# Transposing a row-scaled kernel matrix as two fp16 parts, with fewer warming products and one norm product

## The reference

```python
W = adj * adj
x = layernorm(x + einsum('bnf,nm->bmf', x, W) + bias)      # first layer; its result is called h below

z_l = h @ W_lang.T;  z_g = h @ W_grav.T;  v = h @ W_V.T     # second layer
zn  = z_l / max(norm(z_l), EPS)
A_l = max(zn @ zn.T, 0) * not_eye
A_g = exp(-d2(z_g) / (2 * sigma * sigma)) * not_eye         # d2: squared distances, at least 0
K   = w_l * row_stochastic(A_l * mask) + (1 - w_l) * row_stochastic(A_g * mask)
x   = layernorm(h + (K @ v) @ W_O.T)
```

## Time and profile before

| | |
|---|---|
| time, median of 3 runs | 602.76 us (602.34 to 603.36) |
| the profiled execution, its own time | 602.72 us |
| its span in the profile | 600.9 us |
| PE busy | 588.3 us (98%) |
| PEld busy | 314.3 us (52%) |
| DVE busy | 466.2 us (78%) |
| ACT busy | 275.8 us (46%) |
| POOL busy | 206.3 us (34%) |
| granted TensorE clock, mean of the span | 0.996 |
| first load of x_in, issued and landed | 3.84 us and 10.6 us after the start |

### The profile page before, as it was taken

One profiled execution on the slowest core, in us unless ns is written; L12 is line 12 of the kernel. 1 busy time (PEld: TensorE's weight loads), 2 busy tenths in 40 slices (PEclk: granted clock), 3 DMA queues, 4 the chain that ended last, 5 costly groups with the idle time before them and its releaser, 6 DMA issues.

```text
span 600.9 us, 14104 instructions
## 1 busy us (share of the span) xinstructions
PE 588.3 (98%) x5554; PEld 314.3 (52%) x5554; DVE 466.2 (78%) x964; ACT 275.8 (46%) x473; POOL 206.3 (34%) x200
## 2 busy tenths in 40 slices
PE   9999899999999999999999999999999999999993
PEld 6544555555464555546455555546455555546451
DVE  1756778787878878787887878787887878786775
ACT  2544434445435454444445454544545444533543
POOL 1221604334350624425260523525161533414011
PEclk9999999999999999999999999999999999999998
DMA  8660232324434342233434242233434230314103
GB/s 264 202 183 1 58 85 37 105 86 58 140 70 140 61 123 60 81 103 61 140 70 140 52 111 72 58 126 70 140 70 140 44 96 20 55 71 71 71 2 140
DMA packets 89401, 55.19 MB, mean 92 GB/s; under 512 B 70816, under 2 KB 70816, under 8 KB 89376
## 3 DMA queue, kind: packets, MB, share of 16 engines
q1 hardware_dynamic: 89376, 54.84, 33.3%
HBM read 21.27 MB, written 16.78 MB: 63 GB/s over the span
## 4 chain that ended last, share of the span: by engine, by line
PE 97%; DVE 1%; ACT 1%; issue 0%; POOLq 0%; POOL 0%; ACTq 0%
PE proj L406 35%; PE proj L424 28%; PE front L383 8%; PE ps_t L438 8%; PE ps_v L451 3%; PE ps_t L458 3%; PE ps_k L488 2%; PE front L488 2%; PE proj L572 2%; PE proj L604 2%; PE ps_v L469 2%; PE ps_t L572 1%; PE ps_k L367 1%; PE ps_t L604 1%; PE front L501 0%; DVE stats L937 0%
## 5 line engine op out<-in xcount | busy, mean ns | idle before, releaser
L630 ACT ACTIVATE p_hi<-proj 128x512 f16<-128x512 f32 x128 | 76.1, 595 | 120.1 <-PE proj L406 119.2
L1156 POOL TENSOR_TENSOR x_lo<-x_in,x_hi 128x512 fp32r<-128x512 f32 x60 | 78.6, 1322 | 97.9 <-ACT x_hi L620 97.9
L424 PE MATMUL proj<-m_hi,ht_hi 128*64 128x512 f16 x512 | 98.6, 382 | 0.0
L424 PE MATMUL proj<-m_lo,ht_hi 128*64 128x512 f16 x512 | 97.9, 379 | 0.0
L424 PE MATMUL proj<-m_hi,ht_lo 128*64 128x512 f16 x512 | 97.9, 379 | 0.0
L816 DVE TENSOR_TENSOR p_lo<-proj,p_hi 128x512 f16<-128x512 f32 x128 | 85.8, 680 | 13.5 <-ACT p_hi L630 13.4
L1150 POOL TENSOR_TENSOR ve<-mv,eps_ln 128x4 f32<-128x4 f32 x31 | 12.1, 391 | 166.8 <-DVE mv L789 164.5
L635 ACT ACTIVATE uv<-proj 128x512 f16<-128x512 f32 x64 | 38.1, 595 | 52.5 <-PE proj L424 52.1
L406 PE MATMUL proj<-ht_hi,l_lang_hi 128*128 128x512 f16 x160 | 61.1, 382 | 0.0
L406 PE MATMUL proj<-ht_hi,l_grav_hi 128*128 128x512 f16 x160 | 61.1, 382 | 0.0
L667 ACT ACTIVATE o<-o,nmr,rstd 128x512 f32<-128x512 f32 x60 | 47.0, 808 | 30.1 <-DVE nmr L897 29.7
(11 more groups left out here) (186 smaller groups left out, 1207.7 us busy)
## 6 DMA issues: line engine op xcount, KB each, us to landing
x_in<-in_x SPq DMA_DIRECT2D x16, 1024.0 KB, 6.7
out<-o SPq DMA_DIRECT2D x15, 1024.0 KB, 5.2
w_raw_lang<-in_L_gnn_W_lang SPq DMA_DIRECT2D x4, 256.0 KB, 3.5
o<-in_L_gnn_W_O SPq DMA_DIRECT2D x1, 1024.0 KB, 9.9
w_raw_grav<-in_L_gnn_W_grav SPq DMA_DIRECT2D x4, 256.0 KB, 9.9
uv<-in_L_gnn_W_V SPq DMA_DIRECT2D x1, 1024.0 KB, 12.0
ht_hi<-h_hi SPq DMA_TRANSPOSE x64, 2.5
ht_lo<-h_lo SPq DMA_TRANSPOSE x64, 2.5
```

The lines of the kernel that those rows point to most:

```text
L424: mm = pe.matmul(proj[j % 3][q * N:(q + 1) * N, :], a[g.parity][:, k, rows:rows + N], b[:, k, :], start=(n == 0), stop=(n == len(passes) - 1))
L630: act.activation(p_hi[:, j % 4, :, j // 4, :], by_batch(proj[j % 3]), ACT.Copy).then_inc(phi_ready, 1)
L1156: pool.tensor_tensor(x_lo[:, p, :], x_in[g.parity][:, p, :], x_hi[:, p, :], ALU.subtract).then_inc(xlo_ready, 1)
```

## The change

There are three edits. `WARM_START` goes from 10 to 5. The four accumulating norm products of M become one product with four columns, and DVE adds the four sums before it clamps. And in all groups but the last, `ks_sb` is split into fp16 parts, `ks_hi` on ACT (`ks_high`) and `ks_lo` on DVE (`rows_low`), and `kernel_t` transposes the two parts with fp16 products that accumulate; it waits for the low part. The last group, in `back`, keeps the fp32 products under the name `last_kernel_t`.

```diff
-WARM_START = 10
+WARM_START = 5
...
+        ks_hi = sb("ks_hi", [P, ROWS], F16)
+        ks_lo = sb("ks_lo", [P, ROWS], F16)
+        eye2_16 = sb("eye2_16", [P, N], F16)
...
-            def kernel_t(g):
+            def last_kernel_t(g):
 
                 pe.wait_ge(ks_ready, g.count(1, 1))
                 for b in (0, 2, 1, 3, 4, 6, 5, 7):
                     p, q = b // 4 * 2 + b % 2, b // 2 % 2
                     mm = pe.matmul(ps_v[q * N:(q + 1) * N, p * N:(p + 1) * N],
                                    ks_sb[:, b * N:(b + 1) * N], eye2[:, :], start=True, stop=True)
                 mm.then_inc(kt_done, 1)
 
+            def kernel_t(g):
+
+                pe.wait_ge(kslo_ready, g.count(1, 1))
+                for n, part in enumerate((ks_hi, ks_lo)):
+                    for b in (0, 2, 1, 3, 4, 6, 5, 7):
+                        p, q = b // 4 * 2 + b % 2, b // 2 % 2
+                        mm = pe.matmul(ps_v[q * N:(q + 1) * N, p * N:(p + 1) * N],
+                                       part[:, b * N:(b + 1) * N], eye2_16[:, :],
+                                       start=(n == 0 and b in (0, 2)), stop=(n == 1), skip_group_check=True)
+                mm.then_inc(kt_done, 1)
...
             def back(g):
-                kernel_t(g)
+                last_kernel_t(g)
...
                     pe.wait_ge(norm_copied, 1)
-                    for k in range(DC):
-                        mm = pe.matmul(ps_k[:, 2:3], ones[:, :], ssq[:, 2 + k:3 + k], start=(k == 0), stop=(k == DC - 1))
-                    mm.then_inc(norm_done, 1)
+                    pe.matmul(ps_k[:, 2:2 + DC], ones[:, :], ssq[:, 2:2 + DC], start=True, stop=True).then_inc(norm_done, 1)
...
+            def ks_high(g):
+                act.wait_ge(ks_ready, g.count(1, 1))
+                act.activation(ks_hi[:, :], ks_sb[:, :], ACT.Copy).then_inc(kshi_ready, 1)
...
                 p_high(g, 1, first)
+                if has_prev:
+                    ks_high(before)
                 p_high(g, 2, first)
...
+            def rows_low(g):
+                dve.wait_ge(kshi_ready, g.count(1, 1))
+                dve.tensor_tensor(ks_lo[:, :], ks_sb[:, :], ks_hi[:, :], ALU.subtract).then_inc(kslo_ready, 1)
...
             def m_scale():
                 dve.wait_ge(norm_done, 2)
-                dve.tensor_scalar(ssq_all[:, 2:3], ps_k[:, 2:3], TINY, None, ALU.max).then_inc(norm_copied, 1)
+                dve.reduce_sum(ssq_all[:, 2:3], ps_k[:, 2:2 + DC], X_AXIS).then_inc(norm_copied, 1)
+                dve.wait_ge(norm_copied, 2)
+                dve.tensor_scalar(ssq_all[:, 2:3], ssq_all[:, 2:3], TINY, None, ALU.max).then_inc(norm_copied, 1)
...
                 p_low(g, 1)
+                if has_prev:
+                    rows_low(before)
                 p_low(g, 2)
...
             dve.tensor_copy(eye_g[:, :], ident[:, N:P]).then_inc(dve_const, 1)
+            dve.tensor_copy(eye2_16[:, :], eye2[:, :])
...
                 if not has_prev:
-                    pool.wait_ge(norm_copied, 2)
+                    pool.wait_ge(norm_copied, 3)
```

More of the change, by code:

```diff
@@ L248, in resnorm_graph_kernel @@
         ks_ready = sem("ks_ready")
+        kshi_ready = sem("kshi_ready")
+        kslo_ready = sem("kslo_ready")
         kt_done = sem("kt_done")
```

## The result

| | before | after |
|---|---|---|
| time, median of 6 runs | 602.69 us (601.93 to 603.36) | 598.78 us (598.38 to 599.58) |
| the profiled execution, its own time | 602.72 us | 599.46 us |
| its span | 600.9 us | 597.6 us |

The ratio is 0.9938, with a 95% interval of 0.9925 to 0.9951: 3.9 us faster, where 4.3 were forecast (598.4).

What follows compares the result with a forecast made beforehand. The prediction took PE's instruction list to bound the kernel. Its terms, -3.6 (steady iterations), +0.9 (last iteration), -0.7 (norm) and -0.9 (start), sum to -4.3 against 602.72 us: 598.4 us, range 597.2 to 602.6.

Steps and rivals of the forecast that it cites:

- PE's list bounds the kernel: Whole kernel: the chain is 97% PE, so a us taken out of PE's list is a us of the time.
- The 16 fp16 products take half: `kernel_t`: half of 0.52 us, 0.26 us saved for each group, -3.6 us over 14 steady iterations.
- the first rival: `kernel_t`: the pace of the pairs stays, the steady gain goes, 602.3 us; chance 0.18.
- The two new steps hide in the steady iterations: `ks_high` on ACT and `rows_low` on DVE end before PE reaches `kernel_t`: margin 0.18 us, wait 0.
- The last iteration loses 0.9: Last iteration's `kernel_t`: PE waits 1.2 us for the low part, less 0.26 saved, +0.9 us.
- The norm gives 0.7: Norm of M, ahead of `project(0)`: 6 of 8 PE instructions go, -0.7 us.
- The warming products give 0.9: Start: PE begins W_lang's first block earlier, the level rising at the same moment, about 5.4 us: -0.9 us.
- the fourth rival: Start: the level rises later, +0.5 us for the start, all else as forecast, 599.8 us; chance 0.14.
- The sum: All terms against the profiled execution's 602.72 us: -4.3 us, so 598.4 us.

Runs made afterwards that it cites:

- late_low: The changed kernel with `rows_low` behind `p_low(2)` in DVE's list rather than ahead of it: 611.79 us, ratio 1.0157 to before.
- last_fp32_warm_6: The changed kernel with the last iteration's transposition in fp32 again and six warming products rather than five: 598.58 us, ratio 0.9925 to before.
- warm_only: The kernel before with `WARM_START` 5 rather than 10 and nothing else: 602.20 us, ratio 0.9990 to before.
- undo_warm: The changed kernel with `WARM_START` back at 10: 599.99 us, ratio 0.9958 to before.
- changed_again: The changed kernel itself, unaltered, run again on another chip: 599.01 us, ratio 0.9943 to before.
- fp32_unpaired: The kernel before with the blocks of its fp32 `kernel_t` in the order (0, 1, 4, 5, 2, 3, 6, 7): 608.03 us in a single execution.

## Why the prediction was right, point by point

- **PE's list bounds the kernel**: right. Every us of the result can be read as a us of that list: fewer transposition steps, fewer norm steps, an earlier start, one wait.
- **The 16 fp16 products take half**: right, and the first rival is out. They take 0.25 us against some 0.47. The term was mis-sized a little: -3.15 us and not -3.6. I put 0.10 of the 0.62 us down to the gap behind the products, and halved 0.52. The eight pairs of before are 8 x 0.058 = 0.47, and the gap behind fp32 products is about 0.15; the eight pairs of fp16 are 8 x 0.032 = 0.25, and some 0.12 is left of the gap. The weight load's row, 110 ns against 137, and 110 to 113 in the changed kernel, was the right one to go by. Whether the load or the product set the pace of 0.058 in fp32 is argued from the earlier trace rows, and no run separates the two. The Trainium skill's rule in "TensorE: Matmul & The Clock Gate", "LDWEIGHTS (loading the stationary operand)", gives 53 ns for these loads. Here a pair of loads and products passes every 0.032 us, so for 64 fp16 columns the measurement decides against it. The Trainium skill's floor of some 25 ns between starts ("TensorE: Matmul & The Clock Gate", under "Wait — 56ns, not 53.3ns?") doesn't hold across two halves either: 16 products start within 0.25 us.
- **The two new steps hide in the steady iterations**: right. The room forecast was 0.18 us, and 0.2 is there; `late_low` shows that this wait is the one that decides, and that it was thin.
- **The last iteration loses 0.9**: right, 0.97, and `last_fp32` gives it back.
- **The norm gives 0.7**: right, 0.66. DVE's second small instruction cost nothing that shows: ACT's `p_high(0)` now follows on M's split without idle time, and the first `gram`'s wait of 1.5 us is the same.
- **The warming products give 0.9**: right on average, not in a single execution. I assumed that the level rises at 5.4 us in both kernels. By the spacing of the products it rose at 5.6, 6.4, 6.9, 7.1 and 7.3 us in the five profiles with ten warming products (mean 6.7), and at 5.8 to 7.3 in the seven with five (mean 6.6). So 5.4 was not the moment, but the two kernels do share one on average, and that is all that the term needs: W_lang's first block starts 1.9 us earlier (3.57 and 5.48), so 1.9 us more of it run at half speed ahead of the rise, and that is half of 1.9 us of its work, 0.95, wherever the rise is. The 7.0 against 6.4 us that the expectation of `last_fp32_warm_6` starts from come from the lengths of the first block, which with five products hold the first load's delay and the last product's tail as well. By the spacing there was no later rise to explain. The first layer of group 0 starts at 15.12 on average in the former (14.62 to 15.42), at 14.15 in the latter (13.66 to 14.57): 0.97 us. The profile of before happened to be the earliest of its kind, which is why the two profiles differ by 0.43 only: between these two the fourth rival, a later rise, came near (599.46 us, where it had 599.8). That the averages agree so well with so few profiles, each spread over 0.8 to 0.9 us, is in part luck. In the times, `warm_only` gives 0.4, `undo_warm` against the changed kernel 1.0 to 1.2 (on other chips).
- **The sum**: -3.15 + 0.97 - 0.66 - 0.97 = -3.8, measured -3.9, and -3.4 with `changed_again` on another chip (medians). The forecast of -4.3 was high by the transposition's half us.

What stays open: the executions of one kernel spread over 0.7 to 1.7 us. Between the two profiled ones of the changed kernel the start is all that differs (583.4 us from the first layer to the end in both), but it isn't shown that it explains the whole spread. The profile of before has the earliest rise of its kind, and yet that execution took 602.72 where the fastest took 601.88. By the start alone that would need a rise 1.7 us earlier, at 3.9 us (an estimate, twice the 0.84 us), and no profile shows one before 5.6. Why the moment varies is open too.

A version better than both kernels comes out of it: `last_fp32`, the change with the last iteration's transposition left in fp32, at 598.40 and 598.15 us (0.9930 and 0.9921 of before). That it is better than the changed kernel rests on the marks (0.96 us), not on the medians.

## What to carry to other kernels

A step inserted into a full pipeline costs what its consumer waits, not what it lasts: 1.3 us of new work for each group was free where two us of room stood, cost a wait of 1.1 us in the one iteration where they didn't, and would have cost 0.7 in each with two DVE instructions in the other order. So look at the iterations with a missing part (the first, the last) apart from the steady ones; the best version treats them apart too. And take the parts of a small gain from marks inside the traces (a period, the distance of two stages), which agree to 0.01 to 0.03 us, rather than from times that spread over 1 us and more.

## What the runs showed of the hardware

- The moment at which PE rises to 2.4 GHz varied between executions with the same start of the program (5.6 to 7.3 us with ten warming products, 5.8 to 7.3 with five), while the granted clock was shown as 1.00 throughout. The level could be read only from the spacing of like products (128 columns in fp32: 0.213 and 0.111 us) and from their loads (0.34 and 0.19). With no work ahead of 3.44 us it was 8.5.
- Products of 64 columns of weights and 64 of data on alternate halves pass in pairs, 0.032 us a pair in fp16 and 0.058 in fp32, each with its own weight load. In `fp32_unpaired`, where the order doesn't alternate, the halves still overlap, the first product of the second half passing three older ones (inferred from the starts).
- A kernel whose PE waits 0.64 us in each iteration (`late_low`) ran three of four times at a mean granted clock of 0.992, and 1.7 to 2.0 us slower than at 0.996. Whether the wait is the cause isn't shown.
